# A decoder layer on one core: attention scores on two half-height row tiles of TensorE instead of zero-padded keys

## What is computed

```
q_hk   = (x @ Wq.T)                      # 16 heads
q_big  = einsum('bshk,hkq->bshq', q_hk, w_kc_q); q_big = rope(q_big)       # 192 wide
kv_r   = rope(ctx)                                                         # 8 x 128 x 64
q_r    = einsum('bshq,hqr->bhsr', q_big, W_qr)
k_r    = einsum('bld,hdr->bhlr', kv_r, W_kr)
scores = einsum('bhsr,bhlr->bhsl', q_r, k_r)
attn   = softmax(scores)
ctx_c  = einsum('bhsl,bld->bhsd', attn, kv_r)
out    = ctx_c, through w_kc_kv and Wo
```

## Time and profile before

| | us |
|---|---|
| median of 3 runs | 578.58 |
| lowest, highest | 576.97, 579.41 |
| span of the profiled execution | 576.9 |

### The profile page before, as it was taken

The page is one execution under the profiler, slowest core; times in us unless marked ns, Lnnn a source line. Parts: engine busy times, 40 slices in busy tenths (PEclk is TensorE's granted clock), DMA queues, the critical chain, the costliest instruction groups (busy, mean ns, idle before and its releaser), DMA issues.

```text
span 576.9 us, 9884 instructions
## 1 busy us (share of the span) xinstructions
PE 514.2 (89%) x2964; PEld 355.6 (62%) x2972; DVE 410.4 (71%) x748; ACT 298.3 (52%) x723; POOL 240.2 (42%) x158
## 2 busy tenths in 40 slices
PE   5999966998988988989999999999999999999733
PEld 2438765443433433434788888888888888888522
DVE  0947897489999999998455566767676676767543
ACT  1639748986676676773143253524535352453510
POOL 3211472478888888882222322221232223123010
PEclk9999978999999999999999999999999999999875
DMA  8612583411111110112000000000000000000000
GB/s 313 265 73 58 163 254 147 191 38 38 36 36 29 35 45 18 45 45 77 19 1 1 9 2 2 19 0 18 0 18 0 0 18 0 18 0 18 0 10 9
DMA packets 16194, 29.88 MB, mean 52 GB/s; under 512 B 1712, under 2 KB 10288, under 8 KB 15216
## 3 DMA queue, kind: packets, MB, share of 16 engines
q1 hardware_dynamic: 16176, 29.64, 15.1%
HBM read 23.34 MB, written 6.29 MB: 51 GB/s over the span
## 4 chain that ended last, share of the span: by engine, by line
PE 63%; DVE 18%; issue 11%; ACT 3%; DMA 2%; DVEq 1%; POOL 1%; SPq 0%; POOLq 0%; ACTq 0%
PE ps L355 57%; DVE ps L1071 10%; PE ps L546 3%; DVE reg_b L1082 3%; DMA reg_a<-w_kr 1%; DVE x1T L1031 1%; DMA reg_c<-x_fm 1%; PE ps L473 1%; DVE zs_t L1088 1%; DVE small L1092 1%; DVE x L1107 1%; PE ps L431 1%; ACT x1T L694 1%; ACT reg_b L798 0%; PE ps L596 0%
## 5 line engine op out<-in xcount | busy, mean ns | idle before, releaser
L921 POOL TENSOR_TENSOR reg_b<-reg_c,reg_a 128x1024 f32<-128x1024 f32 x56 | 131.8, 2365 | 32.0 <-DVE reg_b L1078 17.8
L355 PE MATMUL ps<-reg_b,diag 128*128 128x512 f32 x256 | 122.4, 605 | 10.6 <-DVE reg_b L1082 9.6
L938 POOL TENSOR_TENSOR reg_b<-reg_b 128x768 f32<-128x768 f32 x32 | 58.0, 1811 | 145.6 <-DVE reg_b L1130 145.6
L355 PE MATMUL ps<-x1T,Mw 128*128 (+1 forms) x768 | 93.3, 278 | 0.0
L355 PEld LDWEIGHTS ps<-x1T,Mw 128*128 128x128 f32 x768 | 88.4, 192 | 4.6 <-issue 4.4
L355 PEld LDWEIGHTS ps<-reg_b,diag 128*128 128x128 f32 x256 | 43.9, 189 | 75.4 <-issue 42.0
L714 ACT ACTIVATE ps<-reg_b 128x512 f32<-128x512 f32 x112 | 67.2, 600 | 36.7 <-DVE reg_b L1082 35.9
L1071 DVE TENSOR_TENSOR ps<-ps,reg_b 128x512 f32<-128x512 f32 x112 | 76.7, 689 | 8.4 <-ACT ps L714 8.2
L1082 DVE SCALAR_TENSOR_TENSOR reg_b<-reg_c,bc,ps 128x512 f32<-128x512 f32 x112 | 81.7, 735 | 0.0
L355 PE MATMUL ps<-reg_b,Nw 128*128 128x128 f32 (+1 forms) x512 | 64.1, 294 | 0.6 <-POOL reg_b L938 0.6
L355 PEld LDWEIGHTS ps<-reg_b,Nw 128*128 128x128 f32 (+1 forms) x512 | 46.7, 162 | 14.4 <-issue 5.5
(11 more groups left out here) (142 smaller groups left out, 736.1 us busy)
## 6 DMA issues: line engine op xcount, KB each, us to landing
reg_a<-a_log SPq DMA_DIRECT2D x4, 1024.0 KB, 6.0
reg_a<-w_q SPq DMA_DIRECT2D x1, 2048.0 KB, 11.3
zs_dram<-reg_c SPq DMA_DIRECT2D x4, 512.0 KB, 2.8
ud_dram<-Nw SPq DMA_DIRECT2D x4, 512.0 KB, 4.9
reg_a<-w_o SPq DMA_DIRECT2D x1, 2048.0 KB, 11.1
ud_t<-ud_dram SPq DMA_DIRECT2D x8, 256.0 KB, 2.7
zs_t<-zs_dram SPq DMA_DIRECT2D x8, 256.0 KB, 2.7
reg_a<-w_kcq SPq DMA_DIRECT2D x1, 1536.0 KB, 14.5
```

What stands on the lines that cost most here:

```text
L355: return pe.matmul(o, l, r, start=start, stop=stop)
L921: pool.tensor_tensor(dA[:, g % RING], delta_r[:, bass.ds(t, 1), :].to_broadcast([P, SA, DI]), Abc[:, g * SA:(g + 1) * SA, :], ALU.mult).th ...
L938: pool.tensor_tensor(rq[:, g % 2].rearrange("p a c n -> p (a c n)"), pc[:, g % 2].rearrange("p a c n -> p (a c n)"), psn[:, g % 2].rearran ...
```

## The change

- The keys are kept once for each half, without zeros: `kvT`, 128 columns for a batch element, with the same keys on partitions 0-63 and on 64-127. A buffer `ff_raw` of its own takes the second half of the raw FFN weights. GpSimd's memset of `kv_eo` and its semaphore go; VectorE makes one copy of 128 partitions where it made two of 64.
- `scores` has four matmuls in place of two. Each has 64 rows: the even head's latents and the keys on partitions 0-63, the odd head's on 64-127, in turn, with 128 columns. Even heads go to bank 2, odd heads to bank 3, 256 columns each.
- The latents move from bank 2 to columns 256 to 511 of bank 5, beside the context in columns 0 to 255. `to_latent` of group k waits for `cte` to reach k - 1 as well: the copy of the context of group k-2 must be done.
- `row_max` reads from two banks, and writes its four results in the heads' old order; `soft` reads head h from bank 2 + h % 2.
- The keys of one batch element are first copied to `kvT_step` by GpSimd (`step_kT`, in slot g = 1 ahead of `rope_sum`, after the scores of the batch element before are done), and the first scores of a batch element wait for it (`kts_s`).

```diff
@@ setup @@
-        kv_eo = sb("kv_eo", [P, T, 2, P])
+        kvT = sb("kvT", [P, T, P])
+        ff_raw = sb("ff_raw", [P, KM * FF])
...
+        kvT_step = carve(P)
...
+        scores_of = ps[:, 2:4, 0:256].rearrange("p e (i n) -> p e i n", i=2)
+        latents_of = ps[:, 5, 256:512]
@@ TensorE @@
             def to_latent(k, g):
                 pe.wait_ge(radd, k + 1)
                 need(pe, qev, k)
-                Q = ps[:, 2, :]
+                need(pe, cte, k - 1)
+                Q = latents_of
...
             def scores(k, t, g):
                 pe.wait_ge(qev, k + 1)
                 need(pe, pexp, k)
+                if g == 0:
+                    pe.wait_ge(kts_s, t + 1)
                 for i in range(2):
-                    last = mm(ps[:, 3, i * 256:(i + 1) * 256], qk[:, g % 2, i, :],
-                              kv_eo[:, bass.ds(t, 1), :, :].rearrange("p t e n -> p (t e n)"))
+                    for e in range(2):
+                        r = slice(e * DC, (e + 1) * DC)
+                        last = mm(scores_of[:, e, i, :], qk[r, g % 2, i, :], kvT_step[r, :])
@@ ScalarE @@
-                act.activation(qk[:, g % 2].rearrange("p i n -> p (i n)"), ps[:, 2, 0:256], ACT.Copy).then_inc(qev, 1)
+                act.activation(qk[:, g % 2].rearrange("p i n -> p (i n)"), latents_of, ACT.Copy).then_inc(qev, 1)
...
-                    last = act.activation(prob[:, g % 2, h, :], ps[:, 3, h * P:(h + 1) * P], ACT.Exp,
+                    last = act.activation(prob[:, g % 2, h, :], scores_of[:, h % 2, h // 2, :], ACT.Exp,
@@ GpSimd @@
-            pool.wait_ge(ffq, 2)
-            pool.memset(kv_eo[:, :, :, :], 0.0).then_inc(kvzero, 1)
...
+            def step_kT(t):
+                need(pool, smm, G * t)
+                pool.sem_inc(pool_passed, 1)
+                pool.tensor_copy(kvT_step, kvT[:, bass.ds(t, 1), :].rearrange("p t n -> p (t n)")).then_inc(kts_s, 1)
...
             def slots(t, proj, merge, ff):
                 for g in range(G):
+                    if proj and g == 1:
+                        step_kT(t)
@@ VectorE @@
-            dve.wait_ge(kvzero, 1)
-            src = flat(("KV", 0)).rearrange("p (t n) -> p t n", t=T)
-            dve.tensor_copy(kv_eo[0:DC, :, 0, :], src[0:DC])
-            dve.tensor_copy(kv_eo[DC:P, :, 1, :], src[DC:P]).then_inc(dve_free, 1)
+            dve.wait_ge(ffq, 2)
+            dve.tensor_copy(kvT[:, :, :].rearrange("p t n -> p (t n)"), flat(("KV", 0))).then_inc(dve_free, 1)
...
-                dve.tensor_reduce(negm[:, g % 2], ps[:, 3, :].rearrange("p (h n) -> p h n", h=HG), AX.X,
+                dve.tensor_reduce(negm[:, g % 2].rearrange("p (i e) -> p e i", e=2), scores_of, AX.X,
```

More of the change, by code:

```diff
@@ L145, in decoder_layer @@
             "p (c t n) -> p c t n", c=CI, t=T)
-        kv_flat = kv_eo[:, :, :, :].rearrange("p t e n -> p (t e n)")
-        wup_raw, wdn_raw = kv_flat[:, 0:1024], kv_flat[:, 1024:2048]
+        wup_raw, wdn_raw = kvT[:, :, :].rearrange("p t n -> p (t n)"), ff_raw[:, :]
         kvdup = diag[:, :, :]
@@ L197, in decoder_layer @@
         kvp = sem("kvp"); kv_ready = sem("kv_ready")
-        nzero = sem("nzero"); wzero = sem("wzero"); kvzero = sem("kvzero"); cst = sem("cst")
+        nzero = sem("nzero"); wzero = sem("wzero"); cst = sem("cst")
         ffs = sem("ffs"); ffq = sem("ffq")
@@ L213, in decoder_layer @@
         pte = sem("pte"); cxm = sem("cxm"); rcp = sem("rcp")
-        nrm = sem("nrm"); kvs_s = sem("kvs_s"); cte = sem("cte")
+        nrm = sem("nrm"); kvs_s = sem("kvs_s"); kts_s = sem("kts_s"); cte = sem("cte")
         st_x1 = sem("st_x1"); om = sem("om"); ln2 = sem("ln2"); rs2 = sem("rs2"); x2_s = sem("x2_s")
```

## The result

| | median us | lowest to highest | runs | profiled execution | its span | mean granted clock of TensorE |
|---|---|---|---|---|---|---|
| before | 577.91 | 576.97 to 579.41 | 4 | 578.58 | 576.9 | 0.968 |
| after | 571.13 | 568.62 to 574.30 | 4 | 572.42 | 570.6 | 0.964 |

The kernel got faster: 0.9886 of the time before, with a 95% interval of 0.9841 to 0.9930. That is 6.8 us less between the medians; 7.8 were forecast. The profiled spans are 6.3 us apart.

A forecast was written before the change was run, and what follows sets the result against it. TensorE (PE) was taken to bound the attention stage. Savings of 5.7 us in steady groups, 1.1 in groups 1 to 4 and 1.0 in the setup made 7.8 off 578.58: 570.8 us, range 568.0 to 576.5.

The forecast's parts named there:

- What bounds the kernel, and the price of a record: Attention stage: PE busy 262.5 of 265.7 us, so its savings count; 128-column records take 0.11 us, 256-column ones 0.216.
- The scores' 0.64 and the entry's 0.10: Scores stage: 0.64 us from first start to context plus 0.10 for entering the new tile shape, 0.74 against 0.96.
- The least of the two bounds: Scores' eight records: least 4 x 0.11 us, two at a time; most 8 x 0.11, no overlap. The least was taken.
- D: Rival, scores: entering row tiles costs nothing, since the columns stay 128; 10.4 us saved, 568.2 us; chance 0.07.
- A: Rival, scores: the two row halves take turns, 1.19 against 0.96 us; slower by 5.1, 583.7 us; chance 0.11.
- B: Rival, scores: a matmul's two passes stay in order, five steps of 0.11 us; 4.7 saved, 573.9 us; chance 0.13.
- C: Rival, scores: loads on the same half uncovered, every pair 0.22 us; slower by 1.8, 580.4 us; chance 0.05.
- The steady groups: Attention groups 5 to 29 and group 0, PE busy on both sides: 26 x 0.22 us saved, 5.7.
- Groups 1 to 4: Attention groups without an FFN step between transposes and scores: 0.27 us saved each, limited by ScalarE's probabilities copy; 1.1 together.
- Groups 30 and 31: Last attention groups: no gain; group 30's maximum waits for quantization, group 31's exponentials for ScalarE's context copy behind the FFN's square.
- What it waits for in return: Attention: probabilities keep 0.22 of 0.44 us, latents' wait is 2.85 clear, GpSimd's extra copies and two-bank reads cost nothing.
- The setup: Setup: one key copy saves 1.2 us, GpSimd's block 2 products start earlier and disturb VectorE less; 1.0 us gained.

The follow-up runs named there:

- experiment 1: The changed kernel run once more, without an edit: 572.22 us, ratio 0.9887 to the kernel before.
- experiment 5: Changed kernel with VectorE's copy of the keys made in two pieces of 64 partitions again: 570.58 us, ratio 0.9874 to the kernel before.
- experiment 6: Changed kernel with GpSimd's two products for channel block 1 ahead of its memset of half of reg_a: 566.79 us, ratio 0.9815 to the kernel before.
- experiment 7: Changed kernel with unused bf16 matmuls added ahead of PE's waits in the phases behind the loop: 566.13 us, ratio 0.9808 to the kernel before.
- Experiment 3: Kernel before with the change's banks, waits and four 128-column scores matmuls, but all 128 rows with zero-padded keys: 577.93 us, ratio 1.0001 to the kernel before.
- experiment 2: Changed kernel with both even-head scores matmuls written first, then both odd-head ones: 570.79 us, ratio 0.9884 to the kernel before.
- experiment 4: Changed kernel with the latents' matmuls ordered by shape, four of 128 columns and then four of 64: 559.18 us, ratio 0.9674 to the kernel before.

## Why the prediction was right, and where it was off

**What bounds the kernel, and the price of a record: right.** The attention stage got shorter by what PE saved in it and nothing came late. From the first to the last projection it is 252.7 us before and 245.6 in each of the five traces that have the changed stages as they are (after, experiments 1, 5, 6, 7), so this gain does not depend on the execution. Experiment 3 shows that neither banks nor waits play a part in it.

**The scores' 0.64 and the entry's 0.10: right to 0.01.** The least of the two bounds held, four pairs at 0.11, and the 0.10 for entering the shape was paid, though only rows and not columns of the tile change (0.21 instead of 0.11 ahead of the first scores). That decides against D, under which entering would have cost nothing, and against the three others by the 0.64 alone: A would have needed 0.88 and its loads, B five steps of 0.11, C pairs 0.22 apart. For C there was a page: the Trainium skill, "TensorE: Matmul & The Clock Gate", section "Part 3: Packing small matmuls — row/col tiling", has weight loads overlap matmuls in flight only where the row group differs. By that rule the second pass of a half would start 0.22 after the first; the trace has 0.11 from pair to pair, so the measurement decides against it for this kernel.

**The steady groups: 5.7 forecast, 6.0 measured.** The 0.22 held where the slot has no transposes in bf16 ahead of the scores. In the one slot of four that has them (the second one above) it is 0.27: from projection to projection it is 10.65 us (410.01 to 420.66), before 10.92 (414.49, to 425.41 in the timeline of before). The old scores took 1.02 to the context there (423.36 to 424.38), not 0.96, most likely because those transposes covered their first weight load less well (no run tests it). I had read the old price in one slot and taken it for all four. Six such groups make the 0.3.

**Groups 1 to 4: right.** 0.28 each against 0.27, and the context starts 0.05 after ScalarE's copy, the hand-over that was forecast.

**Groups 30 and 31: nothing forecast, 0.2 measured.** Group 30 gave nothing. Group 31's exponentials started 0.28 us behind the start of ScalarE's copy of the context, as forecast (540.26 and 539.98). But that copy waited for more than the FFN's square. In the trace of before the context's last record on PE ends at 539.93 and the square at 539.92, so the two limits fell together; and the context comes earlier when the scores ahead of it are shorter. After the change the context's records end at 532.15 and the copy starts 0.54 us behind the square's start (531.73), where it was 0.69 (539.29):

```profile
532.27 0.36 ACT L816 ACTIVATE reg_b<-ps 128x256 f32<-128x256 f32 x1
```

The exponentials start at 532.53, 0.26 behind it. They also wait for VectorE's maximum, which ends 0.19 and 0.23 ahead of them (540.07, 532.30); the traces do not separate the two, but both hang on the scores. The step that was wrong is "itself behind the FFN's square": it left out these limits.

**What it waits for in return: right.** The probabilities kept 0.16 us of their 0.44, the latents' new wait was 2.86 clear in the same slot, and GpSimd's busy time in the stage rose by 3.1 us (69.76 to 72.87) without anyone waiting for it.

**The setup: wrong, 1.0 forecast, nothing measured.** The step that failed is "GpSimd's two products for block 2 would start 1.2 earlier". It followed VectorE's queue back to the copies and stopped there. It did not look at GpSimd's memset (72.33 to 75.84), which ended 0.11 us after the step behind the copies had started. The step is over 0.55 to 0.58 us behind the memset whether it starts 0.1 us ahead of the memset's end or 1.5 (before, after, experiments 5 and 6), so an earlier start brings nothing. The Trainium skill, "SBUF — State Buffer", section "SBUF: two separate sides", describes such a disturbance: VectorE and GpSimd share a pair of ports, whoever starts first has it for the whole instruction, and the other fully blocks. It holds this for VectorE's work in a two-port mode, or with two inputs in SBUF against GpSimd work that reads SBUF. The rows agree with a block: the step ends 0.56 and 0.58 us behind the memset whatever its own start, near its undisturbed 0.69. That the step runs in a two-port mode no row here shows. I had read the disturbance at 88.54, a row of the same kind, and had not asked whether the saved time would run into another one.

**The tail: nothing forecast, 1.5 us lost in the profiled execution, 0.5 gained ahead of the head merge and 2.0 lost in it.** The 0.5 goes with the clock too: before, it fell to the half level 0.25 us after the last transposes of the probabilities had started (543.0), after the change 0.9 us (535.9), so that more of this stretch ran at the full one. The changed stages do not bring the long merge by themselves: it took 3.72 us in experiments 2, 4 and 6, which have them, and 5.72 to 5.84 after and in experiments 1 and 5. Whether they make it more frequent is not shown; the mean clock of the timed runs is 0.964 to 0.973 for the kernel before and 0.963 to 0.973 for the changed one. What decides for how long the half level lasts there stays open; with the stage filled (experiment 7) it doesn't come. The sum of 7.8 was thus 1.0 too large in the setup, 0.6 too small in the attention stage and its end, and blind to a clock that alone moves single runs by several us. That the median lies 0.3 us from the 570.8 forecast owes something to a start value 0.7 us above the later median of before; the change in the medians, 6.8 against 7.8, is the fairer comparison.

## What to carry to other kernels

Two products that use half of the array's rows each ran at once here, with rows, weights and a PSUM bank of their own (whether each needs its own bank no run tests), and the program need not even write them in turn. But every change of tile shape cost about 0.1 us and a weight load that nothing covered, so order a stage's matmuls by shape first (here that was worth more than the packing). Before you book the time of a removed instruction, look on every engine at what overlaps the instruction behind it, since that one may be held by something else until the same moment. Read an old price in each kind of slot, not in one. And before you credit an edit with a difference of medians, compare the traces stage by stage: here up to 3.0 us lay in a tail that the edit did not touch.

## What of the hardware had not been expected

- The two row tiles take their work independently of the order in the program: with four records of the even half ahead of four of the odd one, two records still ran at a time (0.39 us for the first two, 1.24 us for the stage with the context, against 0.38 and 1.23). The second record of a pair started 0.013 us after the first, against 0.007.
- Grouping the latents' matmuls by shape saved 0.35 us in a group of 1.92, with the same 16 records of the same sizes.
- A memset of 64x4096 on GpSimd (3.51 us) stretched a VectorE step of 0.69 us to 2.02 and 2.08, and its products of 128x1024 stretched one of 1.23 us to 3.27.
- In the tail, 16 records of 256 columns took 3.72 us in some executions and 5.72 in others of nearly the same kernel, at a granted clock of 0.99 and 0.63. With matmuls put into PE's waiting time the tail took 46.4 us, against 48.8 to 51.8 without.
